# Four layers on a graph of 64 nodes: another order for the opening, a small second score, and VectorE's low part of an entering chunk moved ahead of r's sums

## What is computed

```python
h = relu(layernorm(x)); x = x + attention0(h)        # 8 heads, masked by adj, with biases
h = relu(layernorm(x)); o = attention1(h) @ w_proj + b_proj
x = x + o + layernorm(o) * gamma + beta               # second attention layer
h = relu(layernorm(x))                                # graph attention
hw = h @ W;  s1 = hw @ a1;  s2 = hw @ a2
e = leaky_relu(s1[:, :, None] + s2[:, None, :]) * adj
x = x + elu(softmax(e) @ hw + beta * hw)
h = relu(layernorm(x))                                # gated recurrence, 3 steps
for _ in range(3):
    av = [adj @ h, adj @ h]
    z = sigmoid(av @ w3.T + h @ u3.T + b); r = sigmoid(av @ w4.T + h @ u3.T + b)
    hv = tanh(av @ w5.T + (r * h) @ u5.T + b); h = (1 - z) * h + z * hv
x = x + h
```

## Time and profile before

| What | Value |
|---|---|
| Median of 3 runs | 1560.04 us |
| Profiled execution, its own time and its span | 1560.94 us, 1558.6 us |
| TensorE busy | 1483.4 us (95%) |
| VectorE busy | 1247.0 us (80%) |
| ScalarE busy | 993.5 us (64%) |
| GpSimd busy | 535.5 us (34%) |

### The profile page before, as it was taken

One profiled execution on the slowest core, in us unless ns is written; L12 is line 12 of the kernel. 1 busy time (PEld: TensorE's weight loads), 2 busy tenths in 40 slices (PEclk: granted clock), 3 DMA queues, 4 the chain that ended last, 5 costly groups with the idle time before them and its releaser, 6 DMA issues.

```text
span 1558.6 us, 45103 instructions
## 1 busy us (share of the span) xinstructions
PE 1483.4 (95%) x18552; PEld 1259.4 (81%) x18552; DVE 1247.0 (80%) x2511; ACT 993.5 (64%) x1793; POOL 535.5 (34%) x622
## 2 busy tenths in 40 slices
PE   4899999899899998899999999999999999999997
PEld 3789998799898887688788788788788788787885
DVE  2788788898899998788888788788788788788766
ACT  3667667677677776666666666566566666666553
POOL 1667677666788886411101101111111111111000
PEclk9999999999999999899999999999999999999999
DMA  9200000002223324100000000000000000000000
GB/s 257 84 3 0 0 0 1 16 17 43 56 54 61 73 56 57 28 1 1 28 1 1 29 1 1 29 1 1 29 1 1 29 1 1 28 2 1 28 2 27
DMA packets 36805, 40.86 MB, mean 26 GB/s; under 512 B 11840, under 2 KB 31808, under 8 KB 36672
## 3 DMA queue, kind: packets, MB, share of 16 engines
q0 software_dynamic: 4608, 16.78, 5.7%
q1 hardware_dynamic: 32064, 22.10, 5.0%
HBM read 13.71 MB, written 8.39 MB: 14 GB/s over the span
## 4 chain that ended last, share of the span: by engine, by line
PE 69%; DVE 16%; issue 5%; POOL 4%; ACT 3%; DMA 1%; SPq 0%; DVEq 0%; POOLq 0%; ACTq 0%
PE ring L99 32%; PE scores L99 22%; PE scores L1563 3%; PE ring L1398 2%; DVE total L989 2%; PE scores L1362 2%; PE ring L1548 2%; PE ring L1603 2%; PE ring L1438 2%; POOL s L530 1%; DVE hv L1224 1%; DVE hv L1222 1%; PE ring L1675 1%; DVE r L1242 1%; DVE stats L961 1%
## 5 line engine op out<-in xcount | busy, mean ns | idle before, releaser
L530 POOL TENSOR_TENSOR s<-s,mx 128x512 f32<-128x512 f32 x128 | 137.6, 1095 | 47.6 <-DVE mx L985 47.6
L536 POOL TENSOR_TENSOR s<-s,rtotal 128x512 f32<-128x512 f32 x128 | 131.7, 1068 | 35.6 <-DVE rtotal L991 35.4
L594 POOL TENSOR_TENSOR r_var_eps<-r_mean_var,eps 128x4 f32<-128x4 f32 x16 | 8.3, 522 | 382.7 <-DVE r_mean_var L1139 382.7
L678 ACT ACTIVATE s<-s 128x512 f32<-128x512 f32 x128 | 78.3, 643 | 73.7 <-POOL s L530 73.6
L1268 DVE TENSOR_TENSOR rhp_lo<-r,rhp_hi 128x1024 fp32r<-128x1024 f32 x48 | 58.8, 1225 | 70.6 <-ACT rhp_hi L861 70.6
L980 DVE SCALAR_TENSOR_TENSOR s<-scores,mask 128x512 f32<-128x512 f32 x128 | 87.1, 680 | 32.6 <-PE scores L1362 32.6
L854 ACT ACTIVATE later_w<-ring 128x512 f32<-128x512 f32 x64 | 34.8, 596 | 115.1 <-PE ring L1603 115.1
L880 ACT ACTIVATE hv<-scores,bias 128x512 f32<-128x512 f32 x96 | 66.2, 690 | 57.8 <-PE scores L99 57.8
L690 ACT ACTIVATE pT<-ring 128x512 f32<-128x512 f32 x128 | 66.1, 602 | 45.4 <-PE ring L1398 45.4
L1233 DVE TENSOR_TENSOR agg_lo<-scores,agg_hi 128x512 fp32r<-128x512 f32 x96 | 61.8, 685 | 41.0 <-ACT agg_hi L836 40.4
L843 ACT ACTIVATE r<-r,bias_half 128x512 f32<-128x512 f32 x96 | 64.3, 717 | 42.8 <-DVE r L1242 42.8
(11 more groups left out here) (296 smaller groups left out, 5184.5 us busy)
## 6 DMA issues: line engine op xcount, KB each, us to landing
x<-beta_less_one POOLq DMA_DIRECT2D x16, 512.0 KB, 4.6
x<-o POOLq DMA_DIRECT2D x16, 512.0 KB, 6.5
out_x<-x SPq DMA_DIRECT2D x16, 512.0 KB, 2.9
x<-in_x SPq DMA_DIRECT2D x1, 6656.0 KB, 29.1
later_w<-in_L_gnn_w_w SPq DMA_DIRECT2D x3, 512.0 KB, 6.3
x<-in_x SPq DMA_DIRECT2D x1, 1024.0 KB, 10.3
stage<-in_L_gnn_w_qkv SPq DMA_DIRECT2D x3, 256.0 KB, 3.1
x<-in_x SPq DMA_DIRECT2D x1, 512.0 KB, 3.9
```

The costliest lines, as they stand in the source:

```text
L530: pool.tensor_tensor(sr, sr, mx[:, r, :].unsqueeze(2).to_broadcast([P, CT * 2, N]), ALU.subtract).then_inc(s_shifted, 1)
L536: pool.tensor_tensor(sr, sr, rtotal[:, r, :].unsqueeze(2).to_broadcast([P, CT * 2, N]), ALU.mult).then_inc(p_ready, 1)
L678: act.activation(s[:, par, r, :, :, :], s[:, par, r, :, :, :], ACT.Exp).then_inc(p_exp, 1)
```

## The change

It has three parts. **The opening**: x's second chunk is a load of its own, ahead of the small loads; three rows of the second attention layer (its output bias, gamma and beta) are loaded last, and `beta_less_one` is made in `body(CHUNKS - 3)`. VectorE takes the statistics of chunk 1 between the low parts of Wq and Wk, and in `body(-1)` and `body(0)` the low part of `hT` ahead of everything else. **The second score**: `wa2` and its four instructions go; s2 is taken from the copied `hw`, by 8 matmuls of 64x64, whose stationary is a column of `hw` spread over 64 columns and whose moving operand is a block of the identity, one bank for each graph. They need all four copies of `hw`, which are now signalled in pairs. **The halves**: VectorE's `enter` stands ahead of `r_sum`.

```diff
-        X_CUTS = [0, 1, 3, CHUNKS]
+        X_CUTS = [0, 1, 2, 4, CHUNKS]
...
+                sp.dma_start(x[:, CT:2 * CT, :], xs[:, CT:2 * CT, :]).then_inc(x_loaded[1], 16)
                 for dst, src in small:
                     sp.dma_start(dst, src).then_inc(small_loaded, 16)
                 sp.dma_start(stage[:, 3, :, :], w0["wo"]).then_inc(w_loaded[3], 16)
-                for n in (1, 2):
+                for n in (2, 3):
                     cut = slice(X_CUTS[n] * CT, X_CUTS[n + 1] * CT)
                     sp.dma_start(x[:, cut, :], xs[:, cut, :]).then_inc(x_loaded[n], 16)
+                for dst, src in second_rows:
+                    sp.dma_start(dst, src).then_inc(second_rows_loaded, 16)
...
-                    act.activation(dst[:, t, :], psum[:, bank + t % 2, 0:WX], ACT.Copy).then_inc(hw_copied, 1)
+                    done = act.activation(dst[:, t, :], psum[:, bank + t % 2, 0:WX], ACT.Copy)
+                    if t % 2 == 1:
+                        done.then_inc(hw_copied, 1)
...
                 def body(i, par, lay):
-                    if exists(i + 2):
+                    opening = isinstance(i, int) and i <= 0
+                    if opening:
+                        rows_low(i + 1)
+                    if exists(i + 2) and not (opening and i == -1):
                         x_stats(i + 2, lay)
...
                     if isinstance(i, int) and i == CHUNKS - 3:
                         split_low(1, range(len(names)))
+                        dve.wait_ge(second_rows_loaded, 16 * len(second_rows))
+                        dve.tensor_scalar(beta_less_one[:], beta[:].unsqueeze(1).to_broadcast([P, CT, D]), 1.0, -1.0,
+                                          ALU.mult, ALU.add)
...
+                    if s.enters is not None:
+                        enter(s.enters, s.other)
                     if not s.last:
                         r_sum(n)
-                    if s.enters is not None:
-                        enter(s.enters, s.other)
...
                 x_stats(0, 0)
-                split_low(0, range(3))
+                split_low(0, [0])
+                dve.wait_ge(stats_ready, 1)
+                x_stats(1, 0)
+                split_low(0, [1, 2])
...
-                def graph_s2(c, psum=ring, bank=2):
-                    pe.wait_ge(hw_copied, c * CT + 3)
-                    product(pe, psum[:, bank, :], moving(wa2), moving(g_hT)).then_inc(s2_ready, 1)
+                def graph_s2(c, psum=ring, bank=2, src=hw):
+                    wait_apart(pe, hw_copied, (c + 1) * FT)
+                    for t in range(CT):
+                        for g in range(2):
+                            own = slice(g * N, (g + 1) * N)
+                            last = pe.matmul(psum[own, bank + g, t * N:(t + 1) * N],
+                                             src[own, t, D + 1:D + 2].to_broadcast([N, N]), ident[own, own],
+                                             start=True, stop=True)
+                    last.then_inc(s2_ready, 1)
```

More of the change, by code:

```diff
@@ L188, in network @@
         g_w = Parts(plan, "g_w", [P, FT, WX], start["stage"] + 4096)
-        wa2 = Parts(plan, "wa2", [P, FT, P], start["stage"] + 8256)
         u_stage = w_stage[:, 0, :, :]
@@ L241, in network @@
         small_loaded = sem("small_loaded")
-        x_loaded = [sem(f"x_loaded{n}") for n in range(3)]
+        second_rows_loaded = sem("second_rows_loaded")
+        x_loaded = [sem(f"x_loaded{n}") for n in range(4)]
         w_hi_ready = sem("w_hi_ready")
@@ L289, in network @@
         small += [(col_bias[:, n, :], load_columns(w0[b])) for n, b in enumerate(("bq", "bk", "bv"))]
-        small += [(out_bias[0][:], spread_rows(w0["bo"], P)), (out_bias[1][:], spread_rows(w1["bo"], P))]
-        small += [(gamma[:], spread_rows(w1["gamma"], P)), (beta[:], spread_rows(w1["beta"], P))]
+        small += [(out_bias[0][:], spread_rows(w0["bo"], P))]
+        second_rows = [(out_bias[1][:], spread_rows(w1["bo"], P)), (gamma[:], spread_rows(w1["gamma"], P)),
+                       (beta[:], spread_rows(w1["beta"], P))]
         later_loaded = sem("later_loaded")
@@ L558, in scale @@
                     if in_second(i - 3, lay):
+                        if isinstance(i, int) and i == CHUNKS + 3:
+                            pool.wait_ge(second_rows_loaded, 16 * len(second_rows))
                         pool.wait_ge(o_n_ready, i - 3 - CHUNKS + 1)
@@ L945, in x_stats @@
                 def x_stats(c, lay):
-                    if isinstance(c, int) and c in X_CUTS[:3]:
+                    if isinstance(c, int) and c in X_CUTS[:4]:
                         dve.wait_ge(x_loaded[X_CUTS.index(c)], 16)
@@ L1085, in body @@
                         mask_and_max(i, par, 1, lay)
-                    if exists(i + 1):
-                        for f in range(FT):
-                            dve.wait_ge(hT_hi_ready, (i + 1) * FT + f + 1)
-                            dve.tensor_tensor(hT.lo[:, f, :], ring[:, f, :], f32(hT.hi[:, f, :]),
-                                              ALU.subtract).then_inc(hT_lo_ready, 1)
+                    if exists(i + 1) and not opening:
+                        rows_low(i + 1)
                     if exists(i):
@@ L1652, in half @@
                     if s.graph_a is not None:
-                        for t in (2, 3):
-                            pe.wait_ge(hw_copied, s.graph_a * CT + t - 1)
-                            graph_product(s.graph_a, t)
+                        pe.wait_ge(hw_copied, s.graph_a * FT + 1)
+                        graph_product(s.graph_a, 2)
+                        graph_product(s.graph_a, 3)
                     if s.graph_b is not None:
@@ L1691, in _ @@
                 pe.wait_ge(g_hT_lo_ready, FT)
-                pe.wait_ge(gw_lo_ready, 2)
+                pe.wait_ge(gw_lo_ready, 1)
                 pe.wait_ge(s_masked, T * R)
                 for t in range(CT):
-                    wait(pe, hw_copied, t - 1)
+                    wait(pe, hw_copied, t // 2)
                     graph_product(0, t, high, 2)
@@ L1706, in _ @@
                 graph_aggregate(0, high, 2)
-                for t in (2, 3):
-                    pe.wait_ge(hw_copied, CT + t - 1)
-                    graph_product(1, t, high, 0)
-                graph_s2(1, high, 0)
+                pe.wait_ge(hw_copied, FT + 1)
+                graph_product(1, 2, high, 0)
+                graph_product(1, 3, high, 0)
+                graph_s2(1, high, 0, hw_next)
                 o_products(T + 1, 1)
```

21 lines of the change are left out of this document (8 added, 13 removed).

## The result

The changed kernel takes 1533.03 us (median of 4 runs, 1531.08 to 1535.84), the kernel before beside it 1560.37 us (1559.12 to 1561.59): ratio 0.9826, 95% interval 0.9809 to 0.9844, 27.3 us less. The forecast was 1533.4. Its profiled execution took 1531.08 us, 1529.3 of it the span, which is 29.3 us less than the span before. That execution is the fastest of its four, so some 2 us of the 29.3 are scatter between executions.

A forecast was written before the change was run, and what follows sets the result against it. TensorE was taken to bound the kernel, holding 69% of the chain. Opening 5.9 + second score 9.0 + halves 11.7 = 26.6 us off 1560.0 gave 1533.4 us; bounds 1529 to 1538, a little over 8 in 10 within 1524 to 1542.

The forecast's parts named there:

- What bounds the kernel: Whole kernel: TensorE holds 69% of the last-ending chain, so only less TensorE work or fewer TensorE waits pays.
- The opening, -6.5 + 0.6 us: Opening: earlier products save 6.5 us, beta_less_one, now bare on the chain, adds 0.6; net gain 5.9 us.
- I count the 24 v products at the lower clock: Opening, chunk 1: after a 3.9 us stop, v's products run at half clock, 5.6 us instead of 2.8.
- the gain is carried: After the opening: TensorE has no waits from 64 us on, so the opening's 6.5 us reaches the end.
- The second score, -9.0 us: s2 in 14 halves: 1.39 us falls to about 0.55, with w5 products at 2.99 against 2.79; 9.0 us saved.
- Rival (a): s2: small matmuls run one behind the other, or the drain is paid on both sides; 1541 us, 8%.
- Rival (d): s2: each small matmul shows its whole latency, 3.5 us against 1.39; 1572 us, 1%; decides at 165 ns per matmul.
- The halves, -11.7 us: Halves with an entering chunk: the final transposes' wait for its low part goes entirely, 0.9 us, 13 times.
- The margin: Halves: the entering low part ends about 879.3 us, w3 products at 879.77; only some 0.4 us to spare.
- Rival (b): Halves: the wait moves and does not go; 1539 us, or 1545 if TensorE waits as long for r; 9%.
- Rival (c): Opening and s2: the clock stays up and s2 costs 0.27 + 0.2 us; 1527 us, 8%.
- Rival (e): Opening: gains nothing because chunk 1's load lands with the others; 1539 us, 3%.

The follow-up runs named there:

- e6_beta: The changed kernel with beta_less_one made in body(2) in place of body(CHUNKS - 3): 1532.51 us, ratio 0.9825.
- e3_opening: The kernel before with the opening part of the change alone: 1552.54 us, ratio 0.9953.
- first-step experiment: The kernel before with the opening alone, but VectorE's new order only in body(-1), not in body(0): 1554.22 us, ratio 0.9962.
- e7_both: The changed kernel with q copied ahead of the exponentials in body(0) and beta_less_one made in body(2): 1527.91 us, ratio 0.9798.
- e11_kfirst: e7_both's kernel with k of chunk 1 also copied in body(0) right behind the last exponential, ahead of chunk 2's norm: 1526.48 us, ratio 0.9788.
- e5_qfirst: The changed kernel with q of chunk 1 copied ahead of the four exponentials in body(0): 1528.85 us, ratio 0.9803.

## Why the prediction was right

**What bounds the kernel**: right. Each of the three parts changed one of the places read from the chain and the list of waits, and gave about what stood there. **The size**: 1533.4 predicted, 1533.0 measured, but two terms were off in opposite directions and partly cancel: by the traces below, the opening gave 1.3 us more, s2 0.9 less, and the halves 0.3 more. An agreement to 0.4 us is luck, where the medians of this one kernel differ by 3 us (1533.0 and 1529.8). The prediction's chances don't fit its wide range either: its cases inside 1524 to 1542 add up to some 95%, not to a little more than 80.

**The opening, -6.5 + 0.6 us: the mechanism right, the size too small.** First product at 15.60 (15.4 predicted), chunk 1's at 30.05 (30.4), v behind the copy of q at 39.49 (39.9). The load of chunk 1 came a little later than assumed, since VectorE's statistics wait until 10.79, and had no effect. The step that was mis-sized is "I count the 24 v products at the lower clock", 5.2 to 5.6 us, with another 0.5 on the bias product. The clock fell only at about 39.9 and was back before 44. v took 4.62 us, the bias product its usual 0.88. So the profiled execution shows 7.8 and not 6.5 us. The lead is the same 7.7 to 8.0 us at every body until 270 us: "the gain is carried" held that far. That TensorE has no waits from 64 us on is right only up to there: before the change it waited twice more for `hT_lo`, 4.7 us in all, between 270 and 310 us, where the chain runs through VectorE. `beta_less_one` costs its 0.60 us there. Another 1.0 us goes by a fall of the clock near 299 us, which the prediction didn't have:

```profile
297.03 1.21 DVE hT_lo L1081 x2
302.94 8.25 PE ring L99 x48
```

```profile
300.00:304.00 4.00, 4.00 (x96) 3.61 (x79) 3.27 (x7) 2.39 (x5) 2.59 (x3) 0.66 0.14 44
```

From the start of `hT_lo` to that of the 48 products it is 5.91 us here, against 4.92 in the kernel before and 4.93 in `e6_beta`, where the clock stays at 1.00. So the lead is 6.0 to 6.1 us from 303 to 372 us. `e3_opening` shows the same fall (0.62 in 300 to 304 us): the rival of its expectation did occur in its trace. In medians the opening gave 7.0 us net, where 5.9 was predicted; the traces give 7.8 - 0.6 = 7.2, less the 1.0 in an execution with that fall. The prediction was also right that the 11 us of chunk 1's products don't reach the end. The first-step experiment goes further: body(0)'s new order brings nothing at the bias product and 0.4 us at 373 us.

**The second score, -9.0 us: right in kind, slightly large.** 0.61 + 0.20 us instead of 0.55 + 0.20, so 1.39 + 2.79 - 0.61 - 2.99 = 0.58 saved, 8.1 us in 14 halves; alone it gave 8.4. Rival (a) had two limbs. Matmuls one behind the other is refuted for this order by the 0.61, and the order of one graph after the other shows what it would have cost, 0.89 and not 1.09. A price on both sides does seem to exist, 0.14 us in front beside the 0.20 behind, but it is far too small for 1541. Rival (d), 165 ns or more per matmul, is far off. The new wait for all four copies of `hw` costs nothing in the halves, as counted: the list has none there. On the change of tiling mode the Trainium skill (TensorEngine Tiling (Array Packing), Tiling Modes, Key Properties) says that it drains TensorE and that different tiles run matmuls in parallel. The runs agree with both, without showing a drain as such, and put numbers to them: 0.20 us behind and 0.14 us ahead of a block of small matmuls, for 16 passes as for 32, and 0.61 against 0.89 us for the two orders.

**The halves, -11.7 us: right.** All 13 waits went. The recurrence's first adjacency product is at 626.49 us and 9.15 us earlier than before, the end of the span 29.3 us earlier: 20.15 us are gained between, and less the 8.1 of s2 this leaves 12.05, 0.93 each (0.9 predicted). Alone the medians give 12.5. The margin was as read: `hp_b_lo` ends at 863.49 + 1.28 = 864.77, and the final transposes start at 865.10. (The 9.15 are 7.2 of the opening and 2 that come and go: 1.0 is lost near 299 us, as said, and 3 are gained behind 372 us. There the two stops told of at the end are 1.1 us shorter than in the kernel before, whose clock also fell in 396 to 400 us (0.64), and the lead is 8.6 us at 410 and still at 550. Where the last 0.6, ahead of 626 us, come from is open.) Rival (b) is refuted twice, by the list of waits and by `r_sum` moved later still at no cost.

**Rival (c)** was half right in its clock (v's products were cheaper than forecast), and wrong about s2. **Rival (e)**, the load, did not occur.

## What to carry to other kernels

When a large earlier start (11 us here) is to be costed, follow it through each engine's queue to the next thing that is not earlier. Here a copy out of the matmul banks, standing behind exponentials, took back a third of it, and the half of the reordering in body(0) brought 0.4 us at most in the traces. Where a wait sits between two engines' written orders, ask which instruction of the releasing engine could go first at the cost of one that has slack: `enter` ahead of `r_sum` gave 12 us for two moved lines, and the test of it is to push the delayed work later still and see whether TensorE waits. Small matmuls in separate quarters of the array are worth alternating (0.61 against 0.89 us here), and a block of them has a fixed price (0.34 us here) beside that of its matmuls, so it pays where it replaces more than both.

## What the runs showed of the hardware

**The clock falls late and after work has begun again.** In the stop from about 35.8 to 39.49 us the granted clock stays at 1.00, and it is at 0.50 from 40 to 42 us, while TensorE is busy. In the kernel before it fell during the stop. The same stop doesn't always do the same: 1.64 and 1.65 us ahead of chunk 1's products left the clock at 1.00 in the changed kernel and in `e7_both`, and in `e11_kfirst` it fell behind 1.65 us. Near 299 us it fell in the changed kernel and not in `e6_beta`. The fall near 299 us costs 1.0 us, so that such falls are one of the things by which the times scatter. In `e5_qfirst` the fall is as in the changed kernel: a stop of 2.58 us until 42.05, then 0.85 in 42 to 44 and 0.50 in 44 to 46.

**Two stops of TensorE without a cause in the program's own waits.** Near 389 and 408 us the chain has "issue" pieces inside one group of matmuls; the same two, first in the changed kernel and then in its second execution:

```profile
389.10 1.53 issue
408.09 1.32 issue
```

```profile
390.10 1.53 issue
409.09 1.87 issue
```

In `e5_qfirst` they are 1.81 and 2.24 us, in the kernel before 2.08 and 1.86. The DMA engines are busy in the same stretch of the changed kernel, where the stretch before it has a share of 0.08:

```profile
388.00:392.00 4.00, 2.46 (x133) 2.08 (x133) 2.88 (x6) 2.48 (x6) 2.96 (x4) 1.00 1.04 198
```

Nearly all of that traffic is the program's own: two transfers of 512 KB into x, which GpSimd issues just before, `x<-beta_less_one` at 386.37 us and `x<-o`:

```profile
387.02 1.15 POOL L559 DMA_DIRECT2D x<-o  x1
```

While such transfers run, one packet of 16 KB goes over the queue that the profile calls "instruction", up to 2 us ahead of or at the start of each of the stops: in the changed kernel between 388 and 389 and between 406 and 407 us, and likewise in the second execution, in `e5_qfirst` and in the kernel before. That fits a load of TensorE's instructions that is late behind the data, but doesn't show it: such a packet beside such a transfer also stands between 374 and 375 us, where TensorE doesn't stop. The place in the program is the same in these four traces. The length changes between executions of one kernel in the second stop (1.32 and 1.87 us) and not in the first (1.53 both times). With the falls of the clock, and the opening, where the second execution's products of chunk 1 start 0.8 us behind those of the first, the stops are what differs in the traces; which of them moved the medians of this kernel by 3 us (1533.0 and 1529.8) is not known.
